# Squares ahead of rotations in the local layers, and seven smaller moves, in a two-layer transformer kernel

## The reference, cut to what matters

```python
x = L0_attn_x                                # 16 batches x 256 positions x 128
xn = _layernorm(x)
x = x + favor_attention(xn) + local_stack(xn)
xn = _layernorm(x)
x = x + attention(xn) + experts(xn)          # 16 heads of 8; 8 experts and a shared one

def _layer(x, wqkv, qs, ksc, wo, lg, lb, w1, b1, w2, b2):     # local_stack runs this twice
    h = shift_token(x)
    q, k, v = to_heads(jnp.split(h @ wqkv, 3, axis=-1))       # 8 heads of 64
    q = l2norm(q) * qs                                        # needs the sum of squares of each head
    k = l2norm(k) * ksc
    q, k = rotary_xpos(q, k)                                  # a*cos - b*sin, b*cos + a*sin, scaled
    x = x + local_attention(q, k, v) @ wo                     # windows of 64, with the one before
    h = layernorm(shift_token(x)) * lg + lb
    a, g = jnp.split(h @ w1 + b1, 2, axis=-1)
    return x + (a * gelu(g)) @ w2 + b2
```

## Time and profile before

| | |
|---|---|
| timed, median of 3 | 2131.61 us (2127.35 to 2134.83) |
| profiled execution, its own time | 2121.56 us |
| its span | 2119.7 us, 43570 instructions |
| TensorE matmuls / weight loads busy | 1836.3 us (87%) / 1073.3 us (51%) |
| VectorE busy | 1311.8 us (62%) |
| ScalarE busy | 765.7 us (36%) |
| GpSimd busy | 272.2 us (13%) |
| granted TensorE clock, mean | 0.946 of full (2.4 GHz) |

### The profile page before, as it was taken

The page is one execution under the profiler, slowest core; times in us unless marked ns, Lnnn a source line. Parts: engine busy times, 40 slices in busy tenths (PEclk is TensorE's granted clock), DMA queues, the critical chain, the costliest instruction groups (busy, mean ns, idle before and its releaser), DMA issues.

```text
span 2119.7 us, 43570 instructions
## 1 busy us (share of the span) xinstructions
PE 1836.3 (87%) x18228; PEld 1073.3 (51%) x18228; DVE 1311.8 (62%) x2760; ACT 765.7 (36%) x1442; POOL 272.2 (13%) x222
## 2 busy tenths in 40 slices
PE   6888988889898888988989889898898888988888
PEld 3545445455355544555445554455544554545544
DVE  5766547665567655775567655676556674466754
ACT  3134252343523434224333244332453324523234
POOL 2010210101101101011010110110102101021010
PEclk9899999999999999999999999999999999999999
DMA  5000100011000100002000020000200002000020
GB/s 184 7 1 12 20 7 7 1 16 17 6 7 2 26 7 6 7 2 28 4 6 7 2 30 2 7 6 3 30 2 12 1 2 30 2 7 1 3 30 7
DMA packets 27766, 29.79 MB, mean 14 GB/s; under 512 B 3685, under 2 KB 26005, under 8 KB 27157
## 3 DMA queue, kind: packets, MB, share of 16 engines
q1 hardware_dynamic: 27572, 27.01, 6.7%
HBM read 12.06 MB, written 2.36 MB: 7 GB/s over the span
## 4 chain that ended last, share of the span: by engine, by line
PE 54%; DVE 26%; ACT 8%; issue 5%; DMA 4%; SPq 4%; ACTq 0%; DVEq 0%
PE bank L762 5%; PE bank L966 5%; PE bank L991 4%; PE bank L981 4%; SPq L453 4%; DMA phi<-parts 3%; DVE ls L1523 3%; DVE ftm L1447 3%; PE bank L794 3%; DVE lc L1505 2%; PE bank L704 2%; ACT phi L1305 2%; PE bank L1004 2%; DVE parts L1457 2%; ACT lc L1305 2%
## 5 line engine op out<-in xcount | busy, mean ns | idle before, releaser
L1686 DVE TENSOR_REDUCE amx<-bank 128x2 f32<-128x512 f32 x256 | 161.9, 685 | 77.1 <-PE bank L1004 77.1
L1271 ACT ACTIVATE silu<-bank 128x512 f32<-128x512 f32 x144 | 84.6, 596 | 284.3 <-PE bank L966 272.0
L1674 DVE TENSOR_TENSOR mh<-bank,silu 128x512 f32<-128x512 f32 x144 | 99.2, 691 | 127.6 <-PE bank L981 120.0
L991 PEld LDWEIGHTS bank<-w_mw,mh 128*128 128x128 f32 x1152 | 137.1, 192 | 25.4 <-issue 25.4
L966 PE MATMUL bank<-xn2T,w_mw 128*128 128x512 f32 x288 | 149.3, 643 | 0.0
L1511 DVE TENSOR_REDUCE lmx<-bank 128x4 f32<-128x512 f32 x128 | 79.5, 685 | 104.6 <-PE bank L762 104.6
L991 PE MATMUL bank<-w_mw,mh 128*128 128x128 f32 x1152 | 143.4, 278 | 0.0
L505 POOL TENSOR_TENSOR xB<-xn2T,lsq 128x512 f32<-128x512 f32 x32 | 40.7, 1272 | 789.7 <-ACT lsq L1277 789.7
L1523 DVE RECIPROCAL ls<-bank 128x256 f32<-128x256 f32 x64 | 112.1, 1751 | 39.8 <-PE bank L814 39.7
L704 PE MATMUL bank<-hT,w_wqkv 128*128 128x512 f32 x256 | 119.1, 603 | 12.1 <-ACT lsq L1182 6.2
L486 POOL TENSOR_TENSOR lc<-lc,ls 128x512 f32<-128x512 f32 x32 | 40.9, 1278 | 626.4 <-DVE lc L1481 626.4
(11 more groups left out here) (292 smaller groups left out, 3722.5 us busy)
## 6 DMA issues: line engine op xcount, KB each, us to landing
phi<-parts SPq DMA_DIRECT2D x96, 64.0 KB
lc<-parts SPq DMA_DIRECT2D x96, 64.0 KB
w_mw<-in_mw SPq DMA_DIRECT2D x3, 1152.0 KB
x_in<-in_x SPq DMA_DIRECT2D x8, 256.0 KB, 2.8
out<-res SPq DMA_DIRECT2D x8, 256.0 KB, 2.3
w_wqkv<-in_wqkv SPq DMA_DIRECT2D x2, 768.0 KB, 6.8
w_w<-in_w SPq DMA_DIRECT2D x1, 682.0 KB, 4.1
mh<-in_rotary SPq DMA_DIRECT2D x1, 512.0 KB, 5.5
```

What stands on the lines that cost most here:

```text
L991: last = mm(bank_of("final")[:, t], mh[:, (2 * q + i) % 4, t], W["mw2"][:, ORDER[q], i, :], start=(q == 0 and j == 0 and i == 0), stop=Fal ...
L1674: V.tensor_tensor(mh[:, n % 4, :], bank_of("moe_u", n)[:], silu[:, n % 2, :], ALU.mult).then_inc(sem["moe_h"], 1)
L1686: V.tensor_reduce(amx[:, 2 * b:2 * b + 2, h], bank_of("att_max", n)[:].rearrange("p (t k) -> p t k", t=2), AX.X, ALU.max).then_inc(sem["at ...
```

## The change

Nothing that is computed changes, only the order and the buffers:

1. Squares get eight buffers, `sq8`: four more in `mh`, which holds nothing at that time. From c = 2 on ScalarE squares a product as soon as it is there, VectorE rotates it after that, and the bank is free at `loc_c`. For c = 0 and 1 the old order stays. `sums(0)` moves ahead of `favor_map(1)`. The exponentials of the second map are split around square 6.
2. VectorE does the favor masks of slot "mean" before it waits for the centred square.
3. The next turn's input is transposed inside `glu_out` of layer 1, after the first hidden chunk, and copied by ScalarE before its table change.
4. ScalarE copies xn2T before x1 and the second early value.
5. The first gate product of expert 2 goes ahead of the first weight broadcast.
6. At the start, the bias products of w1 run before the input's transposes, and VectorE no longer waits for GpSimd's memsets.

```diff
-        sq4 = [lsq[:, 0, :], lsq[:, 1, :], silu[:, 0, :], silu[:, 1, :]]
+        sq8 = [lsq[:, 0, :], lsq[:, 1, :], silu[:, 0, :], silu[:, 1, :]] + [mh[:, i, :] for i in range(4)]
+        SQUARES = ((0, 1, 2, 3, 4, 5, 6, 7), (0, 2, 1, 3, 4, 5, 6, 7))
+
+        def squared(l, c):
+            return 8 * l + SQUARES[l].index(c) + 1
...
-                job("loc_raw", 8 * l + c, "loc_sq", 8 * l + c + 1)
+                job("loc_raw", 8 * l + c, *(("loc_sq", squared(l, c)) if c < 2 else ("loc_c", 8 * l + c + 1)))
...
         job("route_T", 0, "route_T", 1)
+        job("moe_g", 4, "moe_silu", 5)
         weight_job(1)
-        gate_jobs(2)
+        job("moe_g", 5, "moe_silu", 6)
...
             pe.wait_ge(*arrived("first"))
+            bias_products()
             turn_input(0)
-            bias_products()
+            bias_rows()
...
                                 last = mm(bank_of("loc_ss", l)[r0:r0 + 32, :], W["sumrow"][:, g, :], sq8[4 * g + 2 * qk + ab],
...
+                        if p == 2:
+                            if l:
+                                values(0)
+                            sums(0)
                         if l == 0 and p % 2 == 0:
                             favor_map(p // 2)
                         if it and l == 0 and p == 0:
                             att_project(it - 1, 1)
-                        if p == 2:
-                            if l:
-                                values(0)
-                            sums(0)
...
                                 last = mm(o[:, j * P:(j + 1) * P], hid[0:m, c, j * P:(j + 1) * P],
                                           W["w2"][0:m, 1, c, :], start=False, stop=(c == 2), skip_group_check=True)
+                            if c == 0 and it + 1 < TURNS:
+                                turn_input(it + 1)
...
                 if it + 1 < TURNS:
-                    turn_input(it + 1)
                     for j in range(2):
                         early_value(it + 1, j)
...
+                expert_gate(2, (0,))
                 expert_weight(1)
-                expert_gate(2)
+                expert_gate(2, (1,))
...
-                    for c in range(8):
+                    for c in SQUARES[l]:
                         n = 8 * l + c
-                        act.wait_ge(sem["loc_c"], now("loc_c", n + 1))
-                        if c >= 4:
-                            act.wait_ge(sem["loc_ss_ps"], now("loc_ss_ps", 2 * l + 1))
-                        A(sq4[c % 4], bank_of("loc_raw", n)[:], ACT.Square).then_inc(sem["loc_sq"], 1)
+                        if c < 2:
+                            act.wait_ge(sem["loc_c"], now("loc_c", n + 1))
+                        else:
+                            act.wait_ge(sem["loc_raw_ps"], now("loc_raw_ps", n + 1))
+                        A(sq8[c], bank_of("loc_raw", n)[:], ACT.Square).then_inc(sem["loc_sq"], 1)
                         if l == 1 and c == 5:
                             local_value(0)
...
+                        if l == 0 and c == 1:
+                            act.wait_ge(sem["att_pv"], prior("att_pv"))
+                            map_values(0, 4)
+                        if l == 0 and c in (5, 6):
+                            map_values(2 * c - 6, 2 * c - 4)
...
+                    if l and it + 1 < TURNS:
+                        turn_input(it + 1)
                     A(warm[:], W["ident"][:, 0:1], ACT.Exp)
...
                     early_value(it + 1, 0)
+                act.wait_ge(sem["xn2T_ps"], now("xn2T_ps", 1))
+                A(xn2T[:], bank_of("xn2T")[:], ACT.Copy).then_inc(sem["xn2T"], 1)
                 act.wait_ge(sem["xn2"], now("xn2", 1))
...
-            dve.wait_ge(started, 9)
             V.memset(bank[6][:, 0:12], 0.0).then_inc(prep_ps, 1)
...
-                        dve.wait_ge(sem["loc_raw_ps"], now("loc_raw_ps", 2 * m + 1))
                         if p == 0:
+                            dve.wait_ge(sem["loc_raw_ps"], now("loc_raw_ps", 2 * m + 1))
...
+                        else:
+                            dve.wait_ge(sem["loc_sq"], now("loc_sq", squared(l, 2 * p)))
                         V.tensor_tensor(v3(lc[:, c, :]), raw[0], tab(0), ALU.mult)
...
-                        dve.wait_ge(sem["loc_raw_ps"], now("loc_raw_ps", 2 * m + 2))
+                        if p == 0:
+                            dve.wait_ge(sem["loc_raw_ps"], now("loc_raw_ps", 2 * m + 2))
+                        else:
+                            dve.wait_ge(sem["loc_sq"], now("loc_sq", squared(l, 2 * p + 1)))
                         V.tensor_tensor(part[0], raw[1], tab(1), ALU.mult)
...
                     if l == 0:
+                        favor_heads(l, "mean")
                         dve.wait_ge(sem["glu_sq"], now("glu_sq", 1))
                         V.tensor_copy(cen[:], bank_of("glu_mean", l)[:]).then_inc(sem["glu_cen"], 1)
-                    favor_heads(l, "mean")
```

More of the change, by code:

```diff
@@ L524, in bias_products, with bias_rows @@
                                start=True, stop=True)
+            def bias_rows():
                 pe.wait_ge(*arrived("favor"))
@@ L689, in sums @@
                                 r0 = 64 * qk + 32 * ab
-                                last = mm(bank_of("loc_ss", l)[r0:r0 + 32, :], W["sumrow"][:, g, :], sq4[2 * qk + ab],
+                                last = mm(bank_of("loc_ss", l)[r0:r0 + 32, :], W["sumrow"][:, g, :], sq8[4 * g + 2 * qk + ab],
                                           start=(g == 0), stop=(g == 1), skip_group_check=True)
@@ L961, in _, with expert_gate @@
                     early_value(it + 1, 2)
-                def expert_gate(q):
-                    for i in range(2):
+                def expert_gate(q, which=(0, 1)):
+                    for i in which:
                         n = 2 * q + i
@@ L1175, in local_value, with map_values @@
                         A(lv[:, j, :], bank_of("loc_v", n)[:], ACT.Copy).then_inc(sem["loc_v"], 1)
-                    for c in range(8):
-                        n = 8 * l + c
-                        act.wait_ge(sem["loc_c"], now("loc_c", n + 1))
-                        if c >= 4:
-                            act.wait_ge(sem["loc_ss_ps"], now("loc_ss_ps", 2 * l + 1))
-                        A(sq4[c % 4], bank_of("loc_raw", n)[:], ACT.Square).then_inc(sem["loc_sq"], 1)
+                    def map_values(first, last):
+                        for i in range(first, last):
+                            act.wait_ge(sem["favor_map_ps"], now("favor_map_ps", i + 1))
+                            A(phi[:, i, :], bank_of("favor_map", i)[:], ACT.Exp, bias=phibias[:, 0:1]).then_inc(
+                                sem["favor_phi"], 1)
+                    for c in SQUARES[l]:
+                        n = 8 * l + c
+                        if c < 2:
[3 more added lines that the diff above has]
+                        A(sq8[c], bank_of("loc_raw", n)[:], ACT.Square).then_inc(sem["loc_sq"], 1)
                         if l == 1 and c == 5:
                             local_value(0)
[L1185 to L1191, removed]
+                        if l == 0 and c == 1:
[3 more added lines that the diff above has]
+                            map_values(2 * c - 6, 2 * c - 4)
                     act.wait_ge(sem["loc_ss_ps"], now("loc_ss_ps", 2 * l + 2))
@@ L1246, in _ @@
                 if it + 1 < TURNS:
-                    turn_input(it + 1)
-                if it + 1 < TURNS:
                     early_value(it + 1, 0)
+                act.wait_ge(sem["xn2T_ps"], now("xn2T_ps", 1))
+                A(xn2T[:], bank_of("xn2T")[:], ACT.Copy).then_inc(sem["xn2T"], 1)
                 act.wait_ge(sem["xn2"], now("xn2", 1))
@@ L1253, in _ @@
                     early_value(it + 1, 1)
-                act.wait_ge(sem["xn2T_ps"], now("xn2T_ps", 1))
-                A(xn2T[:], bank_of("xn2T")[:], ACT.Copy).then_inc(sem["xn2T"], 1)
                 for i in range(2):
@@ L1398, in _ @@
             input_scale(0)
+            dve.wait_ge(started, 9)
             done = [0]
```

## The result

The changed kernel takes 2078.31 us (median of 4 runs, 2076.06 to 2083.92) against 2133.22 for the kernel before on the same chip (2127.35 to 2135.05): a ratio of 0.9754, interval 0.9729 to 0.9778, 55 us faster. I had forecast 2094 with a range of 2070 to 2118, so the direction and the range held. The profiled execution took 2078.01 (span 2076.2, granted TensorE clock 0.949) against 2121.56 before: 43.5 less.

The account below looks back on a forecast made before the run. No engine is full; a chain handed between engines bounds the kernel. (1.8 + 2.1 + 0.6 + 0.0) x 8 + 2 = 38 us off the 2131.61 median gives 2094, range 2070 to 2118 for 8 in 10.

Parts of the forecast that it names:

- Layer 0, 1.8 forecast: Local layer 0's first part: with early squares and first sums, the second sums start 1.8 us earlier each turn.
- Layer 1, 2.1 forecast: Local layer 1's first part: square 3 and first sums come earlier, so the second sums start 2.1 us earlier each turn.
- Masks, 0.6 forecast: VectorE's favor masks ahead of the centred copy: 0.6 us a turn saved, bounds 0 and 1.2.
- the clock comes back: Rival, chance 0.2: moving the masks restores full clock at the broadcasts and scores, 1.4 us a turn, 11 us: 2083.
- Boundary 0.2 forecast: Turn boundary: earlier input transposes give nothing, copying xn2T before x1 is worth 0.2 us, cancelled by the experts' delay.
- Gate 0 forecast: Experts: TensorE's gain is hidden by the wait for transfers, 0.2 us delay cancels the boundary's 0.2; bounds -0.2 and +0.4 a turn.
- Start 2 forecast: Kernel start: early values begin at 15.1 instead of 17.18, about 2 us saved once, bounds 0 and 4.
- The slower rival: Rival, chance 0.06: longer TensorE idling before the second norm's transposes prolongs half clock, a turn loses 6.3 us: 2144.
- VectorE as the bound in layer 0: Rival, chance 0.15: VectorE's masks end late at 1092.5, the root chain starts only 0.4 us earlier, the turn gains 3.1: 2105.
- The other signs: VectorE's root-chain waits about 0.2 and 1.5 us, ScalarE's 3.27 gone, turns 252 to 259, TensorE's parts wait about 3.

Follow-up runs that it names:

- the version with the late rotation: The changed kernel with GpSimd's last rotation of each local layer waiting until the root chain's roots are made: 2071.89 us, ratio 0.9731.

## Why the prediction was right, and where its sum was off

The two profiles side by side, each stretch added up over the eight turns (us, after less before; the last column is the change of its time at half clock):

| stretch | forecast | measured | half clock |
|---|---|---|---|
| start, to the first product of layer 0 | -2 | -2.0 | 0 |
| layer 0, first product to root chain | -14.4 | -11.8 | -0.2 |
| layer 0, root chain to output projection | 0 | -5.3 | +0.2 |
| layer 0, output projection to layer 1's first product (masks) | -4.8 | -11.5 | -20.5 |
| layer 1, first product to root chain | -16.8 | -17.4 | 0 |
| layer 1, root chain to the reciprocals of L1523 (L1543 after) | 0 | +6.3 | 0 |
| layer 1, from there to the norm's transposes | 0 | -0.9 | -6.1 |
| norm's transposes to the first gate product | 0 | +7.9 | +20.0 |
| from there to the end of the turn | 0 | -8.8 | -10.7 |
| sum | -38 | -43.5 | -17.3 |

The two stretches that the squares act on measure 29 of the 31 us forecast for them, and the mechanism was the one described: that part was right. That the whole came within 6 us of the sum was partly luck, since four terms put at zero measured -5.3, +6.3, +7.9 and -8.8 and cancelled.

- **Layer 0, 1.8 forecast, 1.5 measured** (mean of the turns; 1.6 in the one shown). VectorE's late start and the first sums in TensorE's gap came as written. I had let ScalarE take the second map's exponentials 1.2 us after the map started (1083.5 for 1082.35); they began 1.99 after it, when the last of its matmuls was done. Exponentials, square 6 and product 7 move with that.
- **Layer 1, 2.1 forecast, 2.17 measured.** VectorE's wait there is 1.45, forecast 1.5. Both waits together stand at 14.0 in the list; by the forecast's 0.2 and 1.5 it would be 13.6.
- **What the steps missed.** The sentence "GpSimd's rotations end where they ended and are wanted only behind the root chain" was true and beside the point: they now run *next to* its beginning. That costs 0.73 us a turn in layer 1, 6 us in all; the version with the late rotation gets them back. Squares by the chain are then (1.47 + 2.17 - 0.73) x 8 = 23 us. This is the term that the sum put at nothing with a wrong reason.
- **Masks, 0.6 forecast, 1.4 to 2.0 measured.** The rival "the clock comes back" happened here in part, in addition to the forecast and not in its stead. The profile pair has 1.4 less a turn, with the broadcast at the upper level in five turns of eight and close to it in a sixth. The full 0.6 + 1.4 = 2.0 us a turn shows only beside the late rotation, where all eight are at the upper level: 15.9 us in this stretch, and 17 in the whole kernel. Alone in the kernel before the same edit shows 1.8 us a turn in its own stretches, but 1.0 more behind layer 0's root chain and 1.3 more from the norm's transposes to the end of the turn, both of which run longer at half clock. So what one edit is worth depends on which of the neighbours are in.
- **Boundary 0.2 forecast, about 0.55 by the medians** (4.4 / 8), which the runs don't show clear of the scatter. From the norm's start to the routing product is 0.2 less, as forecast, in the turn shown. Behind it two larger amounts that the forecast didn't have nearly cancel: more half clock ahead of the experts, less waiting for the parts.
- **Gate 0 forecast, 0 measured.** The copy is about 0.2 late (1.87 for 1.63 us) and the wait for the parts hides TensorE's side. **Start 2 forecast, 2.0 measured**: the first product of layer 0 starts at 24.3 instead of 26.3. Between traces of the same start it scatters by up to 1.6.
- **Against the profile's own time** the sum was 38 and the pair gives 43.5. Against the medians it is 55, and that further difference is my starting point: the profiled execution lay 11.7 below the median beside which the change was measured, the profiled one after lay 0.3 below its own. Over 47 timed executions of the kernel before, time and half clock go together: half clock 221 to 269 us, and 0.29 us of time for each. The profiled execution had 229, and I took the saving as the same for every execution. After the change half clock is 212, 212, 246 and 216; with the squares alone it is 166 to 205, mean 190, against a mean of 246. At 0.29 those 56 us would be 16, which with the 23 of the chain makes 39 of the 43 measured. That sum is an estimate; the slope is one of scatter between runs of one kernel, and no experiment set the clock by itself. It doesn't carry over to every change: the edits 3 to 6 alone had 15 us more half clock than the kernel before on their chip and were 5 us faster. The term that was too small is thus most likely the clock, which the forecast had only as a rival of 11 us; that it is the clock is argued and not shown.
- **The slower rival had the clock right and the price wrong.** Its condition came true (3.02 us of standing still before the transposes). In the turn shown, the stretch at half clock behind it is 6.8 us before and after. But before, three of the eight turns had none or 0.5 us; after, all have it. From the transposes to the first gate product that is 1.0 us more a turn, not 6.3, and it was made up behind, so the kernel is not slower. The Trainium skill (TensorE: Matmul & The Clock Gate, section "HAM oscillation — how this bites in real kernels") says that pauses between bursts bring the low clock back; the norm agrees: of the seven turns, four have a piece at half clock there before (behind pauses of 1.0 us), and all seven after (behind 3.02). The rule doesn't explain the gain in the local layers' first parts: they hold 0.2 us of half clock before, none after.
- **VectorE as the bound in layer 0 was wrong**, by little: it is ready 0.3 us ahead of the root chain. The other signs held: VectorE waits 0.29 and 1.45 us, turns last 253.2 to 258.8 us at a clock of 0.94 to 0.96, and TensorE waits 2.7 us for the parts.

The version with the late rotation beats both kernels: 2071.9 us.

## What to carry to other kernels

Where two engines read the same bank, let the one go first whose result others wait for, then move what stood behind it in the same step: here the buffers and the later engine's new order gave nothing without it. When a step comes earlier, look not only for what it waits for but for what it now runs beside. A single profiled execution has a clock of its own; put it beside the clock of the timed runs before a saving is added to their median.

## What the runs showed of the hardware

VectorE's `TENSOR_SCALAR` on 128x64 int32, input and output in SBUF, takes 0.19 to 0.20 us, and 0.91 when issued 0.40 us into a GpSimd `TENSOR_TENSOR` of 128x512 (1.10 in the run that made them overlap on purpose). It ends at 1148.55, right behind GpSimd's 1148.50, and in the other run at 1189.46, right behind 1189.41: it is held until GpSimd is through, not slowed down. Reads from a bank aren't held: `L1508` takes 0.23 beside the same GpSimd instruction, and the rotations, bank and table in, take 0.68 with and without one beside them.

The Trainium skill (SBUF — State Buffer, section "Who interferes with whom") says that VectorE and GpSimd share one pair of ports as an exclusive lock, that whoever issues second is blocked whole, and that `tensor_scalar` can be of the kind that takes the pair; the 0.91 and the 1.10 agree with it.

The last transfers of the parts that lie on the chain, seven after the change, need 7.56 to 10.20 us to land, against 7.41 to 10.84 for eight before. What sets that, and with it about 13 us either way, stays open.
